# Routing of the first six token blocks moved from behind the first attention into it

## The chip, the cores and the metric

The kernel runs on one core of one Trainium2 chip. The metric is the time of one execution on the device in microseconds. The kernel before has a median of 1952.74 us over three runs (1950.49 to 1956.2).

## The reference

Four sequences of 1024 tokens of width 128 go through two layers, each with an attention and a feed-forward part, all added to the running x:

```
x = x + attn0(layernorm(x))   # causal, 16 heads of 8, softmax(q k / sqrt(128)), times Wo
x = x + moe(layernorm(x))     # router: softmax over 8 experts, top 2, weights renormalised
                              # expert: (silu(h @ gate) * (h @ up)) @ down, 128 -> 352 -> 128
x = x + attn1(layernorm(x))   # RMS norm, 16 query heads, 4 key heads, rope factor, not causal
x = x + ffn1(layernorm(x))    # 128 -> 512, a sine term, relu, 512 -> 128
```

The reference is float32. The change touches the place between attn0 and moe: for each token the two experts with the largest probability are found, and only those two are computed for it.

## The kernel before

The 4096 tokens are 32 tiles of 128, in eight blocks of four tiles (GT = 4, NG = 8). Two blocks are one sequence. Blocks 0 to 3 form routing group 0 and blocks 4 to 7 group 1.

**First attention.** It works through 16 head groups, g = 4 b + q: sequence b, heads 4q to 4q+3. While group g is finished, the row maxima of group g+1 and the first eight of g+2 are taken. Each group follows the string ORDERS[0], event by event, the same on TensorE, VectorE and ScalarE:
- "a", 32 per group: one unit of pass A. TensorE writes the scores of 128 queries against the keys up to them (pass_a, L766 and the mask L769). Unit i of eight has 128 (i+1) keys. VectorE takes their row maximum (row_max, L1441). The units use banks 0,1 and 2,3 of PSUM in turn, so pass_a of unit n waits until the row maximum of unit n-2 is taken. Units 0 to 3 of eight are at most 512 wide and so fill only bank 0 or bank 2.
- "b", 48 per group: pass B, the transposed scores with the maximum taken off (L799, L802), in one of three banks, and the exponential by ScalarE (L1179).
- "p", 12 per group: the product with V (pv, L815), four heads at once.
- "c" to "n": the output's copy (L1183), its turn (L831) and its division by the row sum (normalise_out, L1461 and L1466). That of a group's second half stands at the end of the string.

The last group, g = 15, has no pass A left, since there is no next one. Without it banks 0 to 3 are free there.

**Routing.** The dictionary ROUTE says at which step each engine does which part of a block. For group 0's table (key FIRST: blocks 0 to 5) a step below 12 stands at a PV event of the last head group; steps 12 to 25 run after attention(0), in a loop of each engine ("for step in range(LAYERS[0].G, LAST)"). Blocks 6 and 7 (LATE) are routed beside the first 39 expert tiles. The parts of one block are, on TensorE: T1 (turn of the attention output, L706), WO (product with Wo, L914), T2 (turn of the normed rows), LG (router logits, L919), PF (prefix counts, L924 and L926); on ScalarE: CP1, CP2 (copies out of the turn bank, L1210), EX (L1204); on VectorE: ADD (x plus the product, L1512, with the statistics L1356 and L1360), NORM (L1523), SH (L1531, L1534), RA (L1542 to L1550), RB (L1557 to L1566), RC (L1574, L1576), IDX (L1588 to L1594). TA and TB (L1605 to L1628) build the group's table of tiles: which expert each tile of 128 rows has and where its rows begin. Turns go to bank 1, all small results to bank 3.

**GpSimd** first fills the dispatch buffers (18 DMAs, L646, one after each of the first 18 half groups), then works through RS (inverse deviation, L567, L568) and the scatters: for each block 4 for the first choice (SA) and 4 for the second (SB), each an indirect DMA of 128 rows (L577). Blocks 4 and 5 are scattered beside the experts (steps 1, 3, 5, 7), and so are 6 and 7 (14, 16, 19, 21), four in a row each time.

**Experts.** 39 tiles of 128 rows per routing group, 78 in all. SyncE's queue loads a tile's rows and weights (L447, L448), eight tiles ahead at most, and only after the group's table and all its scatters. TensorE turns it (L940), multiplies by gate (L955) and up (L963), turns the product (L973) and multiplies by down (L983). ScalarE scales the result (L1235), and GpSimd scatters it back (L594) from one of four buffers (YS = 4); ScalarE waits for the landing of the scatter of four tiles before.

Most scratch tiles lie in the space of Q, which the attention uses until its end: slot q holds the queries of head group q.

Of the kernel before, what the change touches and what calls it, by code (L numbers as in the profile page):

```python
# [162 lines left out]
def steps(table, offsets, starts):  # L163

    for kind, offset in offsets:
        for u, start in starts.items():
# [4 lines left out]
FIRST = {0: 0, 1: 1, 2: 2, 3: 3, 4: 9, 5: 10}  # L171
LATE = {6: 0, 7: 4}
ROUTE = {
    "tensor": [steps({13: [("TOT", 0)]}, [("WO", 2), ("T2", 5), ("T1", 0), ("LG", 6), ("PF", 9)], FIRST),
               steps({20: [("TOT", 1)]}, [("T1", 1), ("WO", 2), ("T2", 6), ("LG", 7), ("PF", 12)], LATE)],
    "vector": [steps({13: [("TA", 0), ("TB", 0)]}, [("ADD", 2), ("NORM", 4), ("SH", 6), ("RA", 8), ("RB", 8), ("RC", 8), ("IDX", 9)], FIRST),
               steps({21: [("TA", 1)], 22: [("TB", 1)]},
                     [("ADD", 3), ("NORM", 5), ("SH", 8), ("RA", 9), ("RB", 10), ("RC", 11), ("IDX", 13)], LATE)],
    "scalar": [steps({}, [("CP2", 6), ("CP1", 1), ("EX", 7)], FIRST),
               steps({}, [("CP1", 1), ("CP2", 6), ("EX", 8)], LATE)],  # L180
    "gpsimd": [steps({}, [("RS", 2), ("SA", 10), ("SB", 10)], FIRST),
               steps({1: [("SA", 4)], 3: [("SB", 4)], 5: [("SA", 5)], 7: [("SB", 5)], 14: [("SA", 6)], 16: [("SB", 6)],
                      19: [("SA", 7)], 21: [("SB", 7)]}, [("RS", 3)], LATE)],
}
for step, found in ROUTE["gpsimd"][0].items():
    ROUTE["gpsimd"][0][step] = [(kind, u) for kind, u in found if kind == "RS" or u < GU]
LAST = 26
# [12 lines left out]
READS = numbers("vector", ("ADD", "SH", "IDX", "TA"))  # L200
COPIES = numbers("scalar", ("CP1", "CP2"))
assert [({"WO": "ADD", "LG": "SH", "PF": "IDX", "TOT": "TA"}[k], u) for k, u in SMALL] == list(READS)
assert [({"T1": "CP1", "T2": "CP2"}[k], u) for k, u in TURNS] == list(COPIES)
EARLY_TURNS = len(FIRST) * 2
EARLY_SMALL = len(FIRST) * 3 + 1
# [4 lines left out]
def build(nc, h_in, Wqvk, Wo0, router_w, gate_proj, up_proj, down_proj, w_q, w_k, w_v, w_o, g_rms,  # L210
# [9 lines left out]
    with ExitStack() as ctx:  # L220
# [24 lines left out]
        def part(at, *dims):  # L245
# [3 lines left out]
            if len(dims) == 3:  # L249
# [4 lines left out]
        rows = [part(0, GU, GT, ROW), probs[:, :, :].rearrange("p s n -> p (s n)")[:, 0:GU * GT * ROW]  # L254
                .rearrange("p (a b c) -> p a b c", a=GU, b=GT)]
        gated, acts, hT_tile = part(2304, 2, F0), part(3008, 2, F0P), part(3776, 2, P)
        actsT = part(5248, 2, len(FCH), P)
        x_tile, y_tile = part(6144, TS, P), part(4096, YS, P)
        done_e, pick_e = part(7168, TILES, E), part(7168 + TILES * E, TILES, E)
# [42 lines left out]
        tokens2 = sb("tokens2", [P, GT, D])  # L302
# [43 lines left out]
        cmp1 = sb("cmp1", [P, GT, E, E])  # L346
        cmp2 = sb("cmp2", [P, GT, E, E])
# [8 lines left out]
        y = sb("y", [P, GT, D])  # L356
# [68 lines left out]
        def _(sp):  # L425
# [7 lines left out]
            def load_tile(g, t):  # L433
# [97 lines left out]
        def _(pool):  # L531
# [38 lines left out]
            def scatter_rows(u, choice):  # L570

                v = u % GU
                pool.wait_ge(pre["indexed"], u + 1)
                apart(pool)
                for k in range(GT):
                    at = bass.IndirectOffsetOnAxis(ap=index[:, v, choice, k:k + 1], axis=0)
                    pool.indirect_dma_start(dispatch[u // GU][:, :], at, rows[u // GU][:, v, k, :], None)\  # L577
                        .then_inc(scattered[v], 16)

            def route(g, step):  # L580
                for kind, u in ROUTE["gpsimd"][g].get(step, ()):
                    if kind == "RS":
                        inverse(pre["stats"], pre["rstd"], u, rtmp_r[:, u, :], mv_r[:, u, :, 1], rstd_r[:, u, :])
                    else:
                        scatter_rows(u, 0 if kind == "SA" else 1)
# [56 lines left out]
            for n in range(NGRP * (E + 1) * CAP // (FILL * P)):  # L642
                g, c = n % NGRP, n // NGRP
                pool.wait_ge(s[0]["attn_done"], n + 1 + AT_ONE)
                place_of = dispatch[g][c * FILL * P:(c + 1) * FILL * P, :].rearrange("(p r) w -> p (r w)", p=P)
                pool.dma_start(place_of, some).then_inc(filled, 16)  # L646
            pool.wait_ge(filled, 16 * NGRP * (E + 1) * CAP // (FILL * P))
            for step in range(LAST):
                route(0, step)
            pool.wait_ge(s[0]["attn_done"], 2 * NQ + AT_ONE)  # L650
# [51 lines left out]
        def _(pe):  # L702
# [47 lines left out]
            def attention(l):  # L750
# [98 lines left out]
                def batch(b, final):  # L849
                    for q in range(4):  # L850
# [3 lines left out]
                        for ev in hd.events:  # L854
                            if ev[0] == "B":
                                pass_b(g, q, ev[1], ev[2])
                            elif ev[0] == "A":
# [6 lines left out]
                                if more_1:  # L864
                                    borrowed(k, g)
                                if k < 24 and more_1:
                                    pass_a(g + 1, (q + 1) % 4, 1 + k // 8, k % 8)
                                if k >= 24 and more_2:
                                    if k == 24:
                                        quad_loaded(b + (q >= 2), (q + 2) % 4)  # L870
                                    pass_a(g + 2, (q + 2) % 4, 0, k % 8)
                            elif ev[0] == "PV":
                                pv(g, q, ev[1])
                                if final and q == 3 and l == 0:
                                    pe.wait_ge(sl["max_done"], 32 * NQ)
                                    route(0, ev[1])
                                elif final and q == 3 and ev[1] in EARLY["tensor"][l]:
# [18 lines left out]

            def route(g, step):

                first, second = ((1, 3), (6, 7))[g]
                for kind, u in ROUTE["tensor"][g].get(step, ()):  # L900
                    if kind in ("T1", "T2"):
# [4 lines left out]
                        else:  # L906
                            pe.wait_ge(pre["normed"], u + 1)
                            turn(rows[u // GU][:, u % GU, :, 0:D], first, pre["turned"])
# [168 lines left out]

            for step in range(LAYERS[0].G, LAST):
                route(0, step)
# [13 lines left out]
        def _(act):  # L1093
# [61 lines left out]
            def attention(l):  # L1155
# [12 lines left out]
                def batch(b, final):  # L1168
                    for q in range(4):
                        g = 4 * b + q  # L1170
                        for ev in hd.events:
# [13 lines left out]
                            elif ev[0] == "PV" and final and q == 3 and l == 0:  # L1185
                                route(0, ev[1])
# [80 lines left out]
            for step in range(LAYERS[0].G, LAST):  # L1267
                route(0, step)
# [49 lines left out]
        def _(dve):  # L1318
# [116 lines left out]
            def attention(l):  # L1435
# [39 lines left out]
                def batch(b, final):  # L1475
                    for q in range(4):
                        g = 4 * b + q
                        more_1, more_2 = not (final and q == 3), not (final and q >= 2)
                        for ev in hd.events:
# [8 lines left out]
                            elif ev[0] == "PV" and final and q == 3 and l == 0:  # L1488
                                route(0, ev[1])
# [18 lines left out]
            def add_out(u, n, second):  # L1508
# [5 lines left out]
                statistics(u, pre["stats"], mv_r[:, u, :, :])  # L1514

            def norm_rows(u):

                v = u % GU
                dve.wait_ge(pre["rstd"], u + 1)
                if u >= GU:  # L1520
                    dve.wait_ge(s[0]["attn_done"], 2 * NQ + AT_ONE)
                for k in range(GT):
                    last = dve.tensor_scalar(rows[u // GU][:, v, k, 0:D], x[:, u * GT + k, :], mv_r[:, u, k, 0:1],  # L1523
                                             rstd_r[:, u, k:k + 1], ALU.subtract, ALU.mult)
                last.then_inc(pre["normed"], 1)
# [11 lines left out]
            def compare_experts(u):  # L1537

                par = u % 2
                dve.wait_ge(pre["exped"], u + 1)  # L1540
                probs_e = exped[:, par, :, :]
                own.done(dve.tensor_reduce(r1[:, :], probs_e, AX, ALU.add))  # L1542
                own.done(dve.reciprocal(r2[:, :], r1[:, :]))
                own.done(dve.tensor_tensor(rc[:, :, :], probs_e, over_e(r2[:, :]), ALU.mult))
# [36 lines left out]
            def place_rows(u, n, second):  # L1581
# [3 lines left out]
                if u >= GU:  # L1585
                    dve.wait_ge(scattered[v], 16 * 2 * GT)
# [239 lines left out]
```

## Time and profile before

| what | us |
|---|---|
| median of three runs | 1952.74 |
| the profiled execution, device time | 1953.41 |
| its span, first to last instruction | 1951.6 |
| PE busy | 1739.1 (89%) |
| DVE busy | 1380.9 (71%) |
| ACT busy | 1131.4 (58%) |
| POOL busy | 303.0 (16%) |
| mean granted TensorE clock | 0.930 |

PE is TensorE, DVE VectorE, ACT ScalarE, POOL GpSimd, SP SyncE; PEld is the load of weights on TensorE. Busy time leaves out waits. In rows of the timeline the first number is the start, the second the time that the merged instructions took, and the bracket the idle time before them and who ended it. In rows of a stretch the busy time of each engine stands with its count of instructions, then the granted clock (1.00 is 2.4 GHz, 0.50 is 1.2 GHz), the DMA share and GB/s.

### The profile page before, as it was taken

To read this page: it belongs to the slowest core of one execution; us is meant where nothing else is said; L and a number is where in the kernel's file an instruction comes from. 1 tells how busy PE (TensorE), PEld (TensorE's weight loads), DVE (VectorE), ACT (ScalarE), POOL (GpSimd) and SP (SyncE) were. 2 spreads that over 40 slices of the span, in tenths; PEclk is the share of its full clock that TensorE was granted. 3 is DMA by queue.
4 is the path that set the end of the run, shared out by engine and by line. 5 is a ranking of instruction groups with operands and counts; after the bars stand their busy time and mean duration, and the time that the engine had idled before them with its cause. 6 is when DMAs were issued, how large, how long until landed. Compare 5 with 4: busy or idle time off the path is not lost.

```text
span 1951.6 us, 30989 instructions
## 1 busy us (share of the span) xinstructions
PE 1739.1 (89%) x10550; PEld 726.1 (37%) x10550; DVE 1380.9 (71%) x2363; ACT 1131.4 (58%) x2396; POOL 303.0 (16%) x387
## 2 busy tenths in 40 slices
PE   4599999999998456898878999999999999999886
PEld 2234444444443244565521222222222222222365
DVE  6577777777774645446489788888888888884386
ACT  3246666666666123333341677777777777777776
POOL 4100000000001454435350000000000000000265
PEclk9679999999999578899965999999999999999998
DMA  7635443424200011122142011111111111000000
GB/s 212 152 64 120 112 120 111 129 78 50 35 2 2 29 58 50 50 65 66 55 124 32 2 20 19 19 20 18 19 19 20 17 17 17 2 2 1 1 17 27
DMA packets 109098, 96.27 MB, mean 49 GB/s; under 512 B 58478, under 2 KB 86771, under 8 KB 106640
## 3 DMA queue, kind: packets, MB, share of 16 engines
q1 hardware_dynamic: 91104, 48.02, 15.0%
q0 software_dynamic: 10208, 40.39, 5.6%
q10 hardware_dynamic: 7632, 5.88, 1.1%
q8 instruction: 88, 1.44, 0.3%
q14 instruction: 66, 0.54, 0.1%
HBM read 48.03 MB, written 43.38 MB: 47 GB/s over the span
## 4 chain that ended last, share of the span: by engine, by line
PE 73%; issue 8%; DVE 7%; ACT 4%; POOL 2%; DMA 2%; ACTq 1%; another core or an unknown queue 1%; SPq 0%; POOLq 0%; DVEq 0%
PE ps L815 21%; PE ps L799 18%; PE ps L766 18%; DVE rowmax L1441 3%; PE ps L983 2%; PE ps L963 2%; PE ps L955 2%; DMA k_parts<-Q 2%; PE ps L831 2%; ACT probs L1179 2%; PE ps L973 2%; PE ps L769 1%; PE ps L802 1%; ACTq L1096 1%
## 5 line engine op out<-in xcount | busy, mean ns | idle before, releaser
L1441 DVE TENSOR_REDUCE rowmax<-ps 128x1 f32<-128x1024 f32 (+7 forms) x1024 | 970.0, 987 | 245.5 <-PE ps L766 125.1
L1179 ACT ACTIVATE probs<-ps 128x512 f32<-128x512 f32 (+3 forms) x1792 | 857.8, 556 | 345.6 <-PE ps L799 216.5
L766 PE MATMUL ps<-K,Q 72*128 72x512 bf16 (+3 forms) x1792 | 539.6, 376 | 25.3 <-DVE rowmax L1441 21.7
L799 PE MATMUL ps<-Q,K 75*128 75x512 bf16 (+3 forms) x1792 | 537.6, 362 | 12.3 <-ACT probs L1179 8.4
L815 PE MATMUL ps<-probs,V 128*9 128x512 f32 (+3 forms) x3584 | 446.1, 555 | 0.0
L799 PEld LDWEIGHTS ps<-Q,K 75*128 75x128 bf16 x1792 | 166.0, 98 | 361.5 <-ACT probs L1179 263.4
L766 PEld LDWEIGHTS ps<-K,Q 72*128 72x128 bf16 x1792 | 152.7, 99 | 312.8 <-DVE rowmax L1441 164.0
L1661 DVE TENSOR_TENSOR Q<-ps,Q 128x352 f32<-128x352 f32 x78 | 40.9, 524 | 122.5 <-ACT Q L1226 90.5
L567 POOL TENSOR_SCALAR rtmp<-mv 128x4 f32<-128x4 f32 x8 | 1.9, 233 | 808.3 <-DVE mv L1360 808.3
L815 PEld LDWEIGHTS ps<-probs,V 128*9 128x9 f32 x3584 | 61.2, 89 | 146.8 <-ACT probs L1179 84.8
L769 PE MATMUL ps<-causal,identb 128*128 128x128 bf16 x512 | 115.1, 228 | 0.0
L802 PE MATMUL ps<-identb,causal 128*128 128x128 bf16 x512 | 105.3, 223 | 0.0
L1235 ACT ACTIVATE Q<-ps,meta 128x128 f32<-128x128 f32 x78 | 28.6, 367 | 127.0 <-PE ps L983 95.1
L594 POOL DMA_INDIRECT returned<-Q,target x78 | 77.9, 999 | 116.9 <-ACT Q L1235 97.2
L983 PE MATMUL ps<-wd,Q 128*128 (+1 forms) x468 | 68.0, 283 | 4.5 <-issue 3.9
L963 PE MATMUL ps<-wu,Q 128*128 x156 | 66.3, 508 | 0.0
L769 PEld LDWEIGHTS ps<-causal,identb 128*128 128x128 bf16 x512 | 51.6, 101 | 39.3 <-issue 5.5
L1183 ACT ACTIVATE oT<-ps 128x512 f32<-128x512 f32 x64 | 38.4, 600 | 45.7 <-PE ps L815 45.7
L706 PE MATMUL ps<-ident,tokens 128*128 128x128 f32 x128 | 23.1, 310 | 44.9 <-DVE tokens L1393 32.7
L955 PE MATMUL ps<-wg,Q 128*128 x156 | 62.5, 483 | 0.5 <-ACT Q L1218 0.5
L983 PEld LDWEIGHTS ps<-wd,Q 128*128 128x128 f32 (+1 forms) x468 | 60.5, 197 | 6.0 <-issue 5.7
L646 POOL DMA_DIRECT2D dispatch<-wg x18 | 9.7, 536 | 316.8 <-DVE attn L1466 316.8
(226 smaller groups left out, 1484.8 us busy)
## 6 DMA issues: line engine op xcount, KB each, us to landing
dispatch<-wg POOLq DMA_DIRECT2D x18, 1152.0 KB, 8.7
Q<-q_parts SPq DMA_DIRECT2D x288, 64.0 KB
K<-k_parts SPq DMA_DIRECT2D x144, 64.0 KB
q_parts<-Q POOLq DMA_DIRECT2D x16, 384.0 KB, 3.7
Q<-dispatch SPq DMA_DIRECT2D x78, 64.0 KB
probs<-returned SPq DMA_DIRECT2D x8, 512.0 KB
k_parts<-Q POOLq DMA_DIRECT2D x8, 384.0 KB, 7.4
V<-v SPq DMA_DIRECT2D x16, 144.0 KB
```

The source lines that it names most:

```text
L594: pool.indirect_dma_start(returned[:, :], at, y_tile[:, k, :], None, bounds_check=2 * B * S - 1, oob_is_err=False).then_inc(tile_out[k], 16)
L766: last = pe.matmul(buf[:, c:e], Q[0:CROSS, slot, j, i * P:(i + 1) * P], K[0:CROSS, slot, kj, c:e], start=True, stop=not diag)
L769: last = pe.matmul(buf[:, w - P:w], identb[:, :], causal[:, :], start=False, stop=True)
L799: last = pe.matmul(ps[:, bank, c:HALF], K[0:KROWS, q, kj, t * P:(t + 1) * P], Q[0:KROWS, q, j, h * HALF + c:(h + 1) * HALF], start=True, s ...
L802: last = pe.matmul(ps[:, bank, c:c + P], causal[:, :], identb[:, :], start=False, stop=True)
L815: last = pe.matmul(ps[32 * j:32 * j + rows, PV_BANK, c:HALF], V[:, q, t, kj * rows:(kj + 1) * rows], probs[:, (4 * m + j) % PR, c:HALF], s ...
L955: pe.matmul(ps[:, par, 0:F0], hT_tile[:, par, :], wg[:, bass.ds(expert, 1), :].rearrange("p a f -> p (a f)"), start=True, stop=True).then_ ...
L963: pe.matmul(ps[:, 2 + par, 0:F0], hT_tile[:, par, :], wu[:, bass.ds(expert, 1), :].rearrange("p a f -> p (a f)"), start=True, stop=True).t ...
L983: last = pe.matmul(ps[:, 5, P:2 * P], actsT[0:w, n % 2, c, :], wd[0:w, c, bass.ds(expert, 1), :].rearrange("p a d -> p (a d)"), start=(c = ...
L1179: act.activation(probs[:, (4 * m + j) % PR, c:HALF], ps[:, B_BANKS[(4 * m + j) % 3], c:HALF], ACT.Exp, scale=SCALE).then_inc(sl["exp_done" ...
L1441: dve.tensor_reduce(rowmax[:, par, 8 * j + i:8 * j + i + 1], score_a(i % 2)[:, 0:hd.keys(i)], AX, ALU.max).then_inc(sl["max_done"], 1)
L1661: dve.tensor_tensor(acts[:, par, 0:F0], ps[:, 2 + par, 0:F0], gated[:, par, :], ALU.mult)\
```

## The change

"at(window, event)" is a place in pass A of the first attention: event k of 32 of head group g is place 32 g + k, and a window is eight places. EARLY_BLOCKS starts block u at window 32 + 4u, so one block per head group, and a block takes eight windows: the second half of one runs beside the first half of the next. The parts are the same instructions as before, cut finer: ADD loses its statistics to ST and AG, NORM becomes N1 and N2, RA/RB/RC become RA to RF and CA, CB, IDX loses its end to INT, and the table's TA and TB become TA to TG.

```diff
-FIRST = {0: 0, 1: 1, 2: 2, 3: 3, 4: 9, 5: 10}
-LATE = {6: 0, 7: 4}
+def at(window, event):
+    return 8 * window + event
+EARLY_BLOCKS = {0: at(32, 0), 1: at(36, 0), 2: at(40, 0), 3: at(44, 0), 4: at(48, 0), 5: at(52, 0)}
+LATE_BLOCKS = {6: 0, 7: 4}
...
+    "tensor": [steps({at(54, 1): [("TOT", 0)]},
+                     [("T1", at(0, 1)), ("WO", at(1, 1)), ("T2", at(3, 1)), ("LG", at(4, 1)), ("PF", at(7, 1))], EARLY_BLOCKS),
+               steps({21: [("TOT", 1)]}, [("T1", 1), ("WO", 2), ("T2", 6), ("LG", 7), ("PF", 13)], LATE_BLOCKS)],
+    "vector": [steps({at(54, 3): [("TA", 0)], at(54, 5): [("TB", 0)], at(54, 7): [("TC", 0)], at(55, 2): [("TD", 0)],
+                      at(55, 4): [("TE", 0)], at(55, 6): [("TF", 0)], at(56, 2): [("TG", 0)]},
+                     [("ADD", at(1, 3)), ("ST", at(1, 5)), ("AG", at(1, 7)), ("N1", at(2, 4)), ("N2", at(2, 6)),
+                      ("SH", at(4, 3)), ("RA", at(5, 0)), ("RB", at(5, 2)), ("RC", at(5, 4)), ("RD", at(5, 6)),
+                      ("RE", at(6, 0)), ("RF", at(6, 2)), ("CA", at(6, 4)), ("CB", at(6, 6)),
+                      ("IDX", at(7, 3)), ("INT", at(7, 5))], EARLY_BLOCKS),
...
+    "scalar": [steps({}, [("CP1", at(0, 2)), ("CP2", at(3, 2)), ("EX", at(4, 5))], EARLY_BLOCKS),
...
+    "gpsimd": [{}, steps({}, [("RS", 3)] + [(n, 15 + n) for n in range(2 * GT)], LATE_BLOCKS)],
...
+EARLY_ROWS = [("RS", 0), ("RS", 1), ("SC", 0), ("RS", 2), ("SC", 1), ("RS", 3), ("SC", 2), ("RS", 4), ("SC", 3),
+              ("RS", 5), ("SC", 4), ("SC", 5)]
```

On TensorE a routing part follows pass A of its place, and two waits give the banks back before the next wide unit:

```diff
+            def banks_back(step):
+                if step - 3 in TURN_AT:
+                    pe.wait_ge(pre["copied"], TURNS[TURN_AT[step - 3]] + 1)
+                if step - 4 in SMALL_AT:
+                    pe.wait_ge(pre["small_read"], SMALL[SMALL_AT[step - 4]] + 1)
```

VectorE does a part right after the row maximum of its place; ScalarE does one at the place of the "a" in its own order, between exponentials. The loops of steps behind attention(0) go, on all engines. The rows to be scattered get a tensor of their own for two blocks at a time, so a new wait stands before a block is normed:

```diff
+        rows = sb("rows", [P, 2, GT, ROW])
...
+                    if u >= 2:
+                        dve.wait_ge(scattered[(u - 2) % GU], 16 * 2 * GT * ((u - 2) // GU + 1))
```

GpSimd issues its 18 fills in the first 14 half groups ("(g * fills + c) * 7 // 9 + 1"), those of one dispatch buffer before those of the other, then EARLY_ROWS in order with eight scatters for each "SC". Blocks 6 and 7 are scattered one indirect DMA per tile and block, at steps 15 to 22 and 19 to 26. The experts' scratch tiles move into slots 0 and 1 of Q, and SyncE may load the first expert tiles once head group 12 is out of its slot:

```diff
                 if t == 0:
                     sp.wait_ge(pre["tables"], g + 1)
+                    sp.wait_ge(s[0]["o_turned"], 2 * (NQ - 3) + AT_ONE)
```

The comparison tiles cmp1, cmp2 and the table's done_e, pick_e share one tensor; tokens2 and y share the space of rows.

## Rows read from the trace of the kernel before

**Rows 1.** The page: busy tenths of PE and its granted clock in 40 slices.
```profile
PE   4599999999998456898878999999999999999886
...
PEclk9679999999999578899965999999999999999998
```
**Rows 2.** Stretches: one head group; after the last group's middle; layer 1's last group.
```profile
441.20:473.40 32.20, 31.85 (x266) 14.40 (x265) 24.36 (x40) 21.07 (x52) 0.00 (x0) 1.00 0.36 43
...
640.00:704.00 64.00, 21.19 (x129) 15.20 (x125) 44.68 (x199) 6.41 (x18) 35.24 (x38) 0.55 0.11 38
...
1787.10:1834.20 47.10, 41.70 (x243) 13.34 (x241) 7.90 (x33) 35.38 (x69) 2.43 (x4) 1.00 0.00 1
```
**Rows 3.** Timeline: thirtieth half group's division (VectorE), the first expert tile (TensorE).
```profile
601.20 0.29 DVE L1466 TENSOR_TENSOR attn<-ps,rden 128x128 f32<-128x128 f32 x1
...
704.10 0.45 PE L940 MATMUL ps<-ident,Q 128*128 128x128 f32 x1 [2.38 <-DMA meta<-dispatch]
```
**Rows 4.** GpSimd's scatters of rows: duration min/median/max in ns, first and last start.
```profile
L577 POOL DMA_INDIRECT dispatch<-Q,index x32: 957/962/1151, 654.3 to 697.2; - x32
```
**Rows 5.** VectorE's row maxima in 441.2 to 473.4, by width: busy, mean ns, idle before.
```profile
L1441 DVE TENSOR_REDUCE rowmax<-ps 128x1 f32<-128x1024 f32 x4 | 4.9, 1218 | 0.2 <-PE ps L769 0.2
...
L1441 DVE TENSOR_REDUCE rowmax<-ps 128x1 f32<-128x896 f32 x4 | 4.3, 1084 | 0.2 <-PE ps L769 0.2
...
L1441 DVE TENSOR_REDUCE rowmax<-ps 128x1 f32<-128x768 f32 x4 | 3.8, 950 | 0.1
...
L1441 DVE TENSOR_REDUCE rowmax<-ps 128x1 f32<-128x640 f32 x4 | 3.3, 822 | 1.2 <-PE ps L769 1.1
...
L1441 DVE TENSOR_REDUCE rowmax<-ps 128x1 f32<-128x512 f32 x4 | 2.8, 688 | 1.1 <-PE ps L769 1.0
...
L1441 DVE TENSOR_REDUCE rowmax<-ps 128x1 f32<-128x384 f32 x4 | 2.2, 555 | 2.9 <-PE ps L769 2.9
...
L1441 DVE TENSOR_REDUCE rowmax<-ps 128x1 f32<-128x256 f32 x4 | 1.7, 419 | 1.1 <-PE ps L769 1.1
...
L1441 DVE TENSOR_REDUCE rowmax<-ps 128x1 f32<-128x128 f32 x4 | 1.1, 287 | 0.9 <-PE ps L769 0.9
```
**Rows 6.** Waits in 441.2 to 473.4: us in total, times, longest.
```profile
PEld ps L766 <- DVE rowmax L1441: 3.3, 6, 0.9
```
**Rows 7.** Timeline of VectorE: first and last instructions of routing parts.
```profile
610.84 0.69 DVE L1512 TENSOR_TENSOR x<-x,ps 128x512 f32<-128x512 f32 x1 [9.35 <-PE ps L914]
...
612.61 0.38 DVE L1360 BATCH_NORM_AGGREGATE mv_r<-stats 128x2 f32<-128x6 f32 x4
...
621.71 1.08 DVE L1523 TENSOR_SCALAR Q<-x,mv_r,rstd_r 128x128 f32<-128x128 f32 x4
...
647.12 0.19 DVE L1531 TENSOR_REDUCE r<-ps 128x4 f32<-128x32 f32 x1
...
653.26 0.17 DVE L1594 CAST index<-index_f 128x8 int32<-128x8 f32 x1
...
674.63 0.16 DVE L1605 COPY total<-ps 128x8 f32<-128x8 f32 x1
...
680.96 0.18 DVE L1628 TENSOR_SCALAR skip<-t_row 128x39 int32<-128x39 f32 x1
```
**Rows 8.** Timeline of TensorE: a turn, the product with Wo, the logits.
```profile
607.29 0.63 PE L706 MATMUL ps<-ident,attn 128*128 128x128 f32 x4
...
609.64 1.16 PE L914 MATMUL ps<-wo,aT 128*128 128x128 f32 x8
...
627.89 0.96 PE L919 MATMUL ps<-wr,hT 128*128 128x8 f32 x8
```
**Rows 9.** Stretches with the expert turns (L940) alone: PE and PEld with counts, clock.
```profile
719.50:743.60 24.10, 1.19 (x4) 0.56 (x4) 0.91 0.23 63
...
766.50:805.00 38.50, 2.34 (x7) 1.05 (x7) 0.78 0.18 53
805.00:892.00 87.00, 9.88 (x33) 4.52 (x33) 1.00 0.23 61
```

More of the change, by code:

```diff
@@ L185 @@
-for step, found in ROUTE["gpsimd"][0].items():
-    ROUTE["gpsimd"][0][step] = [(kind, u) for kind, u in found if kind == "RS" or u < GU]
-LAST = 26
+    "tensor": [steps({at(54, 1): [("TOT", 0)]},
[7 more added lines that the diff above has]
+                      ("IDX", at(7, 3)), ("INT", at(7, 5))], EARLY_BLOCKS),
+               steps({22: [("TA", 1), ("TB", 1)], 23: [("TC", 1), ("TD", 1)], 24: [("TE", 1), ("TF", 1)], 25: [("TG", 1)]},
+                     [("ADD", 3), ("ST", 3), ("AG", 3), ("N1", 5), ("N2", 5), ("SH", 8), ("RA", 9), ("RB", 9), ("RC", 10),
+                      ("RD", 10), ("RE", 11), ("RF", 11), ("CA", 12), ("CB", 12), ("IDX", 14), ("INT", 14)], LATE_BLOCKS)],
@@ L200 @@
 READS = numbers("vector", ("ADD", "SH", "IDX", "TA"))
+TURN_AT = {step: ev for step, found in ROUTE["tensor"][0].items() for ev in found if ev in TURNS}
+SMALL_AT = {step: ev for step, found in ROUTE["tensor"][0].items() for ev in found if ev in SMALL}
 COPIES = numbers("scalar", ("CP1", "CP2"))
@@ L574, in scatter_rows, with inverse_rows @@
                 apart(pool)
[L575 to L578, printed above, removed]
+                to = bass.IndirectOffsetOnAxis(ap=index[:, v, n // GT, n % GT:n % GT + 1], axis=0)
+                pool.indirect_dma_start(dispatch[u // GU][:, :], to, rows[:, u % 2, n % GT, :], None)\
+                    .then_inc(scattered[v], 16)
+            def inverse_rows(u):
+                inverse(pre["stats"], pre["rstd"], u, rtmp_r[:, u, :], mv_r[:, u, :, 1], rstd_r[:, u, :])
             def route(g, step):
@@ L907, in route @@
                             pe.wait_ge(pre["normed"], u + 1)
-                            turn(rows[u // GU][:, u % GU, :, 0:D], first, pre["turned"])
+                            turn(rows[:, u % 2, :, 0:D], first, pre["turned"])
                         continue
@@ L1076, in _ @@
             attention(0)
-            for step in range(LAYERS[0].G, LAST):
-                route(0, step)
             experts()
@@ L1576, in count_picks @@
+            def count_picks(kind, u):
+                v = u % GU
+                if kind == "CA":
+                    if v == 0:
+                        own.done(dve.memset(count[:, v, 0, :], 0.0))
+                    else:
+                        own.done(dve.tensor_copy(count[:, v, 0, :], count[:, v - 1, GT, :]))
+                for k in ((0, 1) if kind == "CA" else (2, 3)):
                     last = dve.tensor_tensor(count[:, v, k + 1, :], count[:, v, k, :], picked[:, v, k, :], ALU.add)
@@ L1578, in count_picks @@
                         own.done(last)
-                tell(last, pre["picked"], u + 1)
+                    else:
+                        tell(last, pre["picked"], u + 1)
             def place_rows(u, n, second):
```

252 lines of the change are left out of this document (131 added, 121 removed).

## The prediction

> **What bounds the kernel now.** I read first the 40 slices: PE is at 9 tenths in both attentions, and between them stands a hole at the slices from 12 to 16, where PE falls to 4 to 8 tenths and its granted clock with it [rows 1]. Then the stretches. A head group of the first attention takes 32.2 us with PE busy 31.85, VectorE 24.36, ScalarE 21.07 [rows 2]: PE sets the pace there. From 640 to 704 PE is busy 21.2 of 64 us at a mean clock of 0.55 while VectorE works 44.7 and GpSimd 35.2 [rows 2]: that is the routing, alone. Then two single events: group 14 is divided at 601.20, and the first expert tile turns at 704.10 [rows 3], 102.9 us for what is only one more head group and the routing. GpSimd's 32 scatters of blocks 0 to 3 run from 654.3 to 697.2, about 1.3 us each with the gap [rows 4], and the tile loads wait for the last of them, so at the end it is this queue that releases the experts. Last the experts: from 805 on, 33 tiles in 87.0 us, 2.64 each, at clock 1.00; but 4 tiles in 24.1 us and 7 in 38.5 us in two stretches before [rows 9].
>
> **What goes.** The time from 601.20 to 704.10 becomes one bare last group. PE no longer has pass A there, so ScalarE sets it: 48 exponentials and two copies, 21.07 us in a full group [rows 2]. Layer 1's last group, without pass A too, took 47.1 us for 35.4 of ScalarE's work, 1.33 times [rows 2]; the same ratio gives 28, ScalarE alone 21. I take 26.5, and 0.5 for the handover; the tile loads are then long under way, since SyncE's queue has nothing else in the last group, and GpSimd's eight scatters of block 5 end inside it. So the experts start at 628.2 + X, where X is what the moved work adds to groups 8 to 14. Gain here: 704.1 - 628.2 - X = 75.9 - X.
>
> **What it adds to the attention, X.** Per block, on VectorE: ADD, ST and AG from 610.84 to 612.99, 2.15; N1 and N2 1.08; SH, RA to CB, IDX and INT from 647.12 to 653.43, 6.3 with their gaps [rows 7]. Together 9.55 us. VectorE's idle time in a group is 32.2 - 24.36 = 7.8, so that 1.7 cannot fit even if all were used; and it is not all usable. The idle before a row maximum depends on its width: 0.9, 1.1, 2.9, 1.1 and 1.2 us per group (four windows) before units 0 to 4, but 0.1, 0.2 and 0.2 before units 5 to 7 [rows 5]. PE has no spare either: pass A already waits 3.3 us per group for a row maximum [rows 6], and with two buffers each late row maximum is a late pass A, behind which all of pass B and pv stand in PE's fixed order. So I match each piece with the idle behind its place, a fourth of the group's:
> - behind units 4, 5 and 6 stand N1 with CA (1.1), RC (0.9), ST (0.9), INT (0.4), N2 with CB (0.9) and RD (0.65), 4.85 in all, with 0.03 to 0.05 of idle each: 4.6 stays;
> - behind units 0, 2 and 3 stand RA, RE, RB, RF, ADD, SH, IDX, 4.25 in all, with 0.3 each: 2.2 stays;
> - AG behind unit 7, 0.4 against 0.2: 0.2 stays. The widest hole, 0.7 before unit 2, gets no piece.
>
> That is 7.0. On PE a block adds two turns of 0.63, 1.16 for Wo, 0.96 for the logits [rows 8] and, as an estimate, 0.4 for the prefix counts: 3.8. Most of it (the turns, Wo) falls in windows in which VectorE is then the later engine; I let 1.1 of it through. ScalarE's two bank copies and small exponential come between exponentials; with 11 us idle per group it pays them itself. So 8 us per block, 48 for six.
> The table's VectorE work runs from 674.63 to 681.14, 6.5 us [rows 7]; in seven pieces, against the same idle, 5 stays. X = 53. Bounds: below, PE's own work with VectorE's all hidden, 6 x 3.8 = 23; above, nothing hidden and each bank copy as long as a turn waited for: 6 x (9.55 + 3.8 + 1.3) + 6.5 = 94. I stand nearer the middle because of the idle before narrow units [rows 5].
>
> **The new waits.** VectorE's N1 of block u waits for the scatters of block u-2; the row maxima are queued behind it and PE behind them. Block u-2's index is ready at its window 7.6, and N1 comes at 10.5 of the same count: 2.9 windows of some 10 us, 29 us, for eight scatters of 1.3 [rows 4] and an inverse, 12 us. It costs nothing; were that cover gone, each us late would be a us of PE. PE's waits for the banks stand before units 4 and 5, whose pass A waits for the row maximum of unit 2 or 3 anyway; ADD (0.7) may make the one later, and that is in the 7.0. The 18 fills go faster by two ninths, on queues that share the attention's loads; hidden, since PE is at 9 tenths where they run already [rows 1]. GpSimd has 48 scatters in the attention, 62 us, in a queue that was idle there.
> Against hiding GpSimd's work speaks a rule. The slowest of the 32 scatters took 1151 ns, the median 962, though VectorE was busy 44.7 of 64 us at that time [rows 2, 4]. The Trainium skill, page "SBUF — State Buffer", section "SBUF: two separate sides", says that a DMA issued by GpSimd starves while VectorE holds their shared port in a two-port mode, and that 620 ns became about 3100. This case's trace does not show it to that extent. If it held, an estimate by the page's figure puts a block's scatters at some 27 us, just within those 29; the sum would be later by at most a few us per block.
>
> **The experts' first half.** In the stretch from 719.5 to 743.6, four tiles took 24.1 where 2.64 each make 10.6: 13.5 over; from 766.5 to 805 seven took 38.5 instead of 18.5: 20 over [rows 9]. In both GpSimd scatters four rows of a block at a time, 5.1 us, in front of the tiles' own scatters, whose landing frees ScalarE's buffers. The first burst goes (blocks 4 and 5 are done); I leave 3 us for the routing of blocks 6 and 7 there. The second is spread: one extra scatter per tile makes 1.3 + 1.3 = 2.6, the pace of PE, and only in steps 19 to 22, with two, GpSimd is late by 1.3 each, 5 us; with the table 6.5. Gain 33.5 - 9.5 = 24; bounds 15 (bursts cheaper than their stretches look) and 31. Part of it is the clock, which should stay at 1.00.
>
> **Sum.** Span 1951.6 - (75.9 - 53) - 24 = 1904.7. Around the span lie 1953.41 - 1951.6 = 1.8, giving 1906.5 against that execution; the median of the runs was 0.7 less than it, so 1906.
>
> **Rivals.**
> - *The pieces hide.* Routing rides in VectorE's idle and PE's slack, X = 30: 1883. For it: 7.8 us idle per group. Against: the idle is before narrow units, pieces also stand behind wide ones.
> - *Lock-step.* VectorE, PE and ScalarE wait in turn, each part a round trip, X = 80: 1933. For it: two buffers and three banks leave hardly any slack [rows 6]; the old stretch from 640 to 704 shows how such a chain runs. Against: inside the attention other work stands between the parts.
> - *The experts are held up by something else*, for example by GpSimd being late with its chain or by the landing of the scatters: the start gains 20 us less and the spreading only 15 in place of 24: 1935.
> - *The other side: the clock.* The holes that VectorE makes in PE's work let the granted clock fall to 0.50 in the routed groups, as it did behind the attention (0.55 in the mean) [rows 2]. A group's 31.85 + 3.8 of PE work would become up to 71 us in place of about 40, 31 more; 1.5 such groups (46.7 us) eat the gain, beyond 1.7 it is slower than can be told from noise, and two give 1968. For it: PE would be idle about a tenth of the time. Against: 41.70 busy of 47.10 kept a clock of 1.00 [rows 2], and routed groups should have 35.6 of 40.
>
> **How the numbers follow.** My forecast 0.60, hidden 0.13, lock-step 0.16, held up 0.05, clock 0.06. The forecast's own range is 1893 to 1921. The range for 8 in 10 takes in the hidden case and the lock-step: 1881 to 1940. What a measurement of this kernel can tell from no change is about 0.3%, 5.9 us. Faster than 1946.9: all of the first two, nearly all of the third and fourth, 0.91; slower, 0.05 from the clock; 0.04 between, from the tail of lock-step (X above 93).
>
> **What would show it.** Groups 8 to 13 at about 40 us in place of 32.2, group 14 at about 36, groups 0 to 7 as before; in the routed groups pass A's wait for the row maximum well above 3.3 us and VectorE busy about 33 us; PE busy near 36 at clock 1.00. The group 14 division at about 654, the first expert turn 27 us behind it. GpSimd's scatters of blocks 0 to 5 about 1.3 us each, ended before the experts; first 25 expert tiles in about 77 us instead of 101. Wrong would be: routed groups near 36 or above 45, a stretch at 0.50 inside the attention, tile loads later than the last group, a last group other than 24 to 29 us, VectorE found idle before N1 for GpSimd, or waits of 5 us and more for the landing of the experts' scatters, as before.

## The result and the profile after

The change was 1.1% slower: 1973.99 us in the median of four runs (1971.44 to 1982.24) against 1953.18 us (1950.49 to 1956.2) for the kernel before beside it, ratio 1.0113, 95% interval 1.0078 to 1.0149. Forecast was 1906. The profiled execution has a span of 1969.9 us at a mean granted clock of 0.933.

The kernels of one comparison ran on one chip, and the kernel before was run again beside them. That turned out to matter, and the answer stands here in one table; "held" says whether the profiles of that comparison show the stall that the sections below are about.

| comparison | kernel before, us | held | kernels and their ratio to the kernel before (95% interval) |
|---|---|---|---|
| 1 | 1953.18 | yes | the change 1.0113 (1.0078 to 1.0149) |
| 2 | 1952.37 | yes | no_scatter 0.982 (0.9794 to 0.9846); burst_indirect 1.0233 (1.0204 to 1.0261); burst_direct 1.0009 (0.9993 to 1.0026); spread2 0.9861 (0.9837 to 0.9885) |
| 3 | 1954.67 | yes | spread_all 0.9811 (0.9789 to 0.9833); spread_late 0.9815 (0.9767 to 0.9862); burst4 1.0006 (0.9988 to 1.0023); burst_landed 1.0008 (0.9987 to 1.0029) |
| 4 | 1921.23 | no | burst6 1.002 (1.0002 to 1.0038); burst8_half 1.002 (1.0002 to 1.0038); change_landed 1.0027 (1.0014 to 1.004) |
| 5 | 1923.05 | no | the change again, change_b, 0.9874 (0.9843 to 0.9905); burst_indirect_b 0.9987 (0.9963 to 1.0011); burst6_b 1.0022 (1.0005 to 1.004); spread_all_b 0.9845 (0.9819 to 0.9871) |
| 6 | 1923.2 | no | burst6_c 1.0008 (0.9985 to 1.0032); burst8_half_c 0.9994 (0.9973 to 1.0015) |

The page after, which answers to [rows 1]: the hole behind the attention is gone, but PE is now at 7 to 8 tenths in slices 9 to 14 (counted from 0), and PE's clock dips in most of them.
```profile
PE   4599999998878879799977999999999999999887
...
POOL 4100000001111113535360000000000000000265
PEclk9679999998898889899965899999999999999998
```

The stretches, in the columns of [rows 2]. The first is head group 9, the first with a full load of routing; the second is group 10; the third group 14. Each begins some 1.4 us behind the division that ends the group before:
```profile
411.80:451.80 40.00, 35.68 (x292) 16.76 (x292) 32.09 (x80) 22.71 (x55) 3.47 (x5) 1.00 0.29 36
451.80:503.50 51.70, 41.81 (x294) 19.32 (x293) 32.44 (x80) 23.48 (x55) 9.29 (x11) 0.83 0.26 39
...
658.70:706.80 48.10, 36.22 (x245) 14.29 (x245) 24.08 (x59) 20.78 (x51) 12.55 (x14) 0.78 0.09 28
```
Group 9 is as forecast (about 40 us, PE near 36, VectorE about 33, clock 1.00): 40.0 us, PE 35.7, VectorE 32.1, clock 1.00. From group 10 on, with the same work for PE, VectorE and ScalarE, a group takes 51.7, 51.6, 48.6, 55.1 and 48.1 us, at half clock for part of each. What group 10 has and group 9 lacks is POOL's work: 9.29 us against 3.47. GpSimd's first eight scatters start at 449.0, the next eight at 500.6, then 552.2, 600.7, 654.7 and 691.6. Answering to [rows 3], the thirtieth division comes at 705.41 (601.20 before) and the first expert tile at 735.28 (704.10 before):
```profile
705.41 0.29 DVE L1489 TENSOR_TENSOR attn<-ps,rden 128x128 f32<-128x128 f32 x1
...
735.28 0.33 PE L968 MATMUL ps<-ident,Q 128*128 128x128 f32 x1 [0.68 <-DVE attn L1489]
```

The timeline of the second burst shows what happens (start, duration, instruction, and in the bracket the idle time with who ended it):
```profile
505.74 0.22 PE L788 MATMUL ps<-causal,identb 128*128 128x128 bf16 x1
...
507.00 0.95 POOL L588 DMA_INDIRECT dispatch<-rows,index  x1 [0.30 <-issue]
...
508.25 0.96 POOL L588 DMA_INDIRECT dispatch<-rows,index  x1 [0.30 <-issue]
508.64 0.49 ACT L1204 ACTIVATE probs<-ps 128x384 f32<-128x384 f32 x1 [4.78 <-remote]
...
509.19 0.50 PE L818 MATMUL ps<-Q,K 75*128 75x384 bf16 x1 [2.50 <-issue]
...
509.52 0.95 POOL L588 DMA_INDIRECT dispatch<-rows,index  x1 [0.30 <-issue]
512.34 1.16 DVE L1464 TENSOR_REDUCE rowmax<-ps 128x1 f32<-128x384 f32 x2 [8.66 <-remote]
512.42 0.87 ACT L1204 ACTIVATE probs<-ps 128x384 f32<-128x384 f32 x2 [2.80 <-remote]
```
PE's mask product of the 384-wide unit, the last instruction of its pass A, ended at 505.96. VectorE's row maximum of that unit, which waits for it, started at 512.34, 6.4 us later, after 8.66 of idleness that the view can put down to no engine ("remote"). ScalarE has such waits of 4.78 and 2.80 in the same microseconds. The trace also keeps the time of every semaphore update, and there the lateness stands directly. From 440 to 735 PE's updates come 0.01 us behind the end of their instruction in the median, but 33 of 562 come more than 1 us behind it, up to 7.9; of ScalarE's and VectorE's none is 0.1 us late. The rows show it too: ScalarE's exponential ended at 509.13 and PE's next product, which waits for it, began at 509.19, in the middle of VectorE's wait. So what is late is PE's word to the others, and they stand still; I call it the hold. (The ends of matmuls are modelled, so whether the results or only the updates come late is not told apart.) The waits of the whole attention from 440 to 735 (us in total, times, longest), "remote" alone:
```profile
DVE rowmax L1464 <- remote: 33.5, 6, 8.7
...
ACT probs L1204 <- remote: 20.4, 6, 4.8
...
ACT oT L1208 <- remote: 8.4, 1, 8.4
```
In the trace before, no row maximum and no exponential of the attention has such a wait. The granted clock falls to 0.50 (1.2 GHz) 4 to 11 us after the first scatter of each burst: for 17.1, 17.1, 6.8, 13.7, 10.2 and 13.7 us from 457.3, 508.5, 563.1, 610.9, 658.7 and 696.2. One more fall, of 3.4 us at 645.0, stands near no burst. The scatters themselves are as short as in [rows 4]:
```profile
L588 POOL DMA_INDIRECT dispatch<-rows,index x64: 954/958/1122, 449.0 to 832.5; - x64
```

The experts, from the first turn to the start of the 26th: 88.1 us, where the trace before has 103.5 (704.1 to 807.6):
```profile
735.30:823.40 88.10, 7.78 (x25) 3.60 (x26) 0.94 0.16 43
```

### The profile page after: what moved, and what is told of

Its sections match the earlier page's. It is cut to its first block, busy times and chain, and to the rows that moved or that the text cites. A ratio compares the mean times of both kernels' runs of the same rounds, so it can differ in the third digit from the quotient of the medians.

```text
span 1969.9 us, 31128 instructions
## 1 busy us (share of the span) xinstructions
PE 1755.3 (89%) x10550; PEld 723.3 (37%) x10550; DVE 1376.7 (70%) x2363; ACT 1135.5 (58%) x2396; POOL 302.7 (15%) x387
## 4 chain that ended last, share of the span: by engine, by line
PE 69%; DVE 13%; ACT 5%; issue 3%; another core or an unknown queue 3%; POOL 2%; DMA 2%; ACTq 1%; SPq 0%; POOLq 0%; DVEq 0%
PE ps L834 19%; PE ps L818 17%; PE ps L785 17%; DVE rowmax L1464 8%; PE ps L1011 2%; PE ps L991 2%; PE ps L983 2%; ACT probs L1204 2%; DMA k_parts<-Q 2%; PE ps L1001 2%; PE ps L850 2%; PE ps L821 1%; ACTq L1121 1%; PE ps L788 1%
## 5 line engine op out<-in xcount | busy, mean ns | idle before, releaser
L785 PE MATMUL ps<-K,Q 72*128 72x512 bf16 (+3 forms) x1792 | 547.6, 380 | 64.4 <-DVE rowmax L1464 53.8
L818 PE MATMUL ps<-Q,K 75*128 75x512 bf16 (+3 forms) x1792 | 543.8, 365 | 19.7 <-ACT probs L1204 8.6
L1260 ACT ACTIVATE Q<-ps,meta 128x128 f32<-128x128 f32 x78 | 28.6, 367 | 123.5 <-PE ps L1011 87.2
L588 POOL DMA_INDIRECT dispatch<-rows,index x64 | 62.0, 968 | 123.2 <-DVE index L1634 104.5
L1208 ACT ACTIVATE oT<-ps 128x512 f32<-128x512 f32 x64 | 38.4, 600 | 65.3 <-PE ps L834 56.9
L1484 DVE RECIPROCAL rden<-ps 128x16 f32<-128x16 f32 x64 | 16.0, 250 | 68.5 <-PE ps L850 68.3
```

Of the source, the lines that this page charges most:

```text
L588: pool.indirect_dma_start(dispatch[u // GU][:, :], to, rows[:, u % 2, n % GT, :], None)\
L785: last = pe.matmul(buf[:, c:e], Q[0:CROSS, slot, j, i * P:(i + 1) * P], K[0:CROSS, slot, kj, c:e], start=True, stop=not diag)
L818: last = pe.matmul(ps[:, bank, c:HALF], K[0:KROWS, q, kj, t * P:(t + 1) * P], Q[0:KROWS, q, j, h * HALF + c:(h + 1) * HALF], start=True, s ...
```

## Experiments

Theory A: eight indirect DMAs queued by GpSimd hold back the semaphore updates that the other engines wait for, and the clock falls with the hold. Rivals: B, VectorE's routing parts and the waits in lock-step cost it themselves; C, the scatters collide with SyncE's loads; D, any burst of DMAs on GpSimd's queue does it. The expectations use the same letters.

**Take the scatters out.** Blocks 0 to 5 are not dispatched, so the experts work on zero rows; four more fills, to another tensor, make up for the DMAs taken out.
```diff
-                    for n in range(2 * GT):
-                        scatter_rows(u, n)
+                    pool.wait_ge(pre["indexed"], u + 1)
...
-                    if u >= 2:
-                        dve.wait_ge(scattered[(u - 2) % GU], 16 * 2 * GT * ((u - 2) // GU + 1))
```


> The changed kernel without the 48 early scatters of blocks 0 to 5 (the rows of those blocks are not dispatched; four more fills write the return buffer instead, so that it is defined). Theory A, the scatters themselves stop the other engines: groups 10 to 13 come down from 51.6, 51.5, 48.7 and 55 us to about 40, 40, 40 and 46, group 14 to about 39, no wait of 4 us and more on anything in the attention, clock 1.00 there; about 1925 us. Theory B, the parts on VectorE and their round trips cost more than the 8 us per block as soon as two blocks overlap: groups 10 to 13 stay near 50, above 1960 us. Theory C, the scatters collide with SyncE's loads of the next group: as A.

1913.75 us, 0.982. Groups 8 to 14: 35.1, 40.1, 40.1, 41.3, 40.1, 43.7, 35.0 us; no "remote" wait from 440 to 660; first expert tile at 675.9. Two stretches of 40 us, most of groups 9 and 10:
```profile
401.00:441.00 40.00, 36.09 (x299) 16.81 (x291) 31.85 (x75) 23.35 (x57) 1.28 (x2) 1.00 0.30 35
441.00:481.00 40.00, 35.62 (x295) 16.81 (x291) 32.21 (x79) 22.66 (x55) 1.29 (x2) 1.00 0.30 35
```
All routing on VectorE and PE is still there. B falls: with the scatters the first expert tile comes 59 us later (735.3 against 675.9); 3 of these lie before the first division, so 56 are the scatters'.

**Put scatters into the kernel before.** Five bursts of eight, to a scratch tensor, at the starts of groups 10 to 14; the second kernel has the same bytes as direct DMAs.
```diff
+            for b in range(5):
+                pool.wait_ge(s[0]["attn_done"], 2 * (10 + b) + AT_ONE)
+                apart(pool)
+                for k in range(8):
+                    at = bass.IndirectOffsetOnAxis(ap=idx_c[:, k:k + 1], axis=0)
+                    pool.indirect_dma_start(scratch[:, :], at, rows_c, None).then_inc(burst_sem, 16)
+                pool.wait_ge(burst_sem, 16 * 8 * (b + 1))
```
In the second kernel this stands in place of the two lines with "at":
```diff
+                    pool.dma_start(scratch[k * P:(k + 1) * P, :], rows_c).then_inc(burst_sem, 16)
```


> The kernel before, plus five bursts of eight indirect DMAs of 128 rows to a scratch buffer, issued by GpSimd at the start of groups 10 to 14. Nothing waits for them. A: each of these groups goes from 32.3 (30.9 for group 14) to 40 to 44 us, with the same waits of 4 to 9 us on nothing that the profile names; 1995 to 2010 us. B: no change, 1953 us. C: as A in groups 10 to 12, where SyncE loads, and nothing in groups 13 and 14.

> The same five bursts with direct DMAs of the same 128 rows of 576 bytes, also by GpSimd. If what hurts is the indirect kind (A in its narrow form): groups stay at 32.3, 1953 us. If it is any burst on GpSimd's queue, or the collision of its packets with SyncE's loads (C): like the indirect bursts, 1980 us and more. B: 1953 us.

Indirect: 1996.13 us, 1.0233; the five groups took 38.4, 41.7, 43.1, 41.0 and 39.7 us instead of 32.3 and 30.9. Direct: 1954.74 us, 1.0009, groups 32.3 and 30.9 as without. Group 10 with its burst, first indirect (with its "remote" waits), then direct:
```profile
438.70:477.10 38.40, 34.12 (x267) 14.88 (x265) 24.60 (x41) 21.76 (x52) 7.83 (x8) 0.96 0.34 51
...
DVE rowmax L1452 <- remote: 5.1, 2, 3.3
ACT probs L1190 <- remote: 4.5, 1, 4.5
```
```profile
441.90:474.20 32.30, 31.95 (x267) 14.40 (x265) 24.44 (x41) 21.17 (x52) 4.26 (x8) 1.00 0.38 61
```
So the hold needs nothing of the change, and it is not bytes (D falls). C falls too: in groups 13 and 14 SyncE starts one transfer each, at 597 and 638, 34 us behind the first scatter of the burst, and they lost 8.8 and 8.7 us, as much as the others.

**Never eight back to back.** First two units of pass A between scatters, with block 5 left as a burst; then block 5 paced too, by ScalarE's exponentials in the last group (the edit shown); then blocks 6 and 7 at one scatter per tile.
```diff
                     for n in range(2 * GT):
+                        if u < 5:
+                            pool.wait_ge(s[0]["max_done"], 40 + EARLY_BLOCKS[u] + at(7, 6) + 2 * n)
+                        else:
+                            pool.wait_ge(s[0]["exp_done"], 3 + 4 * LAYERS[0].G * (NQ - 1) + 4 + 5 * n)
                         scatter_rows(u, n)
```


> The changed kernel, but GpSimd lets two units of pass A pass between the scatters of a block (eight scatters over 16 units, some 20 us in place of 10). A, if the harm comes from scatters queued back to back: the standstills of 8.7 us per block vanish or shrink to about 1 us, groups 10 to 13 near 42, about 1930 us. A, if each scatter stops the others for its own time: the sum of the stops is the same, about 1970 us. B: no change, 1974 us.

> The changed kernel with two units of pass A between scatters for blocks 0 to 4, as in spread2, and five exponentials of the last group between those of block 5, which in spread2 still went in one burst. If queued scatters are the harm: no wait of 9 us in group 14 or the last group; groups 10 to 13 at 40.1 and 43.7 as in spread2; group 14 35 to 45 (its half clock of 23.9 us in spread2 followed a wait of 4.0 us that may come again), last group 28; 1908 to 1918 us. If the parts on VectorE were at fault in group 14: 1925 us as spread2.

> spread_all, and in the experts' first half blocks 6 and 7 are scattered one after the other, one indirect DMA per tile at steps 15 to 30, never two. If queued scatters cost there too (intervals of 5.2, 5.8, 4.1 and 6.8 us against 2.64 in spread2), the first 39 tiles take 4 to 8 us less than in spread_all; if the two per tile only delay the tiles' own scatters, about 3 us less.

spread2: 1925.03 us, 0.9861; groups 10 to 13 at 40.1 to 43.7, and block 5's burst in group 14 still made one wait of 9.1 us of ScalarE on "remote", group 14 being 52.9. spread_all: 1914.93 us (1910.69 to 1915.09), 0.9811, faster than both kernels; groups 9 to 12 at 40.1, group 13, which has the table too, at 44.9, group 14 at 36.2, no "remote" wait from 440 to 735, first expert tile at 676.5. The same 48 scatters run in it. Groups 10 and 11:
```profile
445.00:485.10 40.10, 35.75 (x291) 16.81 (x291) 32.19 (x81) 22.76 (x54) 9.21 (x11) 1.00 0.34 49
485.10:525.20 40.10, 35.75 (x291) 16.83 (x291) 32.19 (x81) 22.76 (x54) 9.04 (x11) 1.00 0.34 50
```
POOL's 9.2 us are as in the change's group 10, and the 51.7 us are 40.1. spread_late: 1914.21 us, no gain over spread_all (39 expert tiles in 127.0 us against 127.1): its experts still had seven "remote" waits of ScalarE, 22.6 us, the longest 3.5. There a block's scatter stands behind the tiles' own, one by one, and some hold remains; so eight in a row are not the only thing that brings it, and what does in the experts is open.

**How many, and queued or landed.** Bursts of four in the kernel before; eight, each issued when the one before has landed.


> The kernel before plus five bursts at the start of groups 10 to 14, as in burst_indirect, but of four indirect DMAs each. If each indirect DMA costs the other engines its share, the five bursts cost half of burst_indirect's 43.8 us: 1974 us. If the harm comes only once several are queued (the first waits in burst_indirect begin some 4 us after its first DMA), four cost little: groups 32.3 to 34 us, 1953 to 1960 us.

> The five bursts of eight indirect DMAs, but each one is issued only when the one before has landed. If it is their standing in the queue behind each other that stops the others: groups stay at 32.3 us (30.9 for group 14), 1953 us. If it is the number of them in a short time, whatever the order: near 1996 us, or in between as the pace is slower.

burst4: groups 33.0, 33.5, 33.5, 32.6, 31.3 us, 3.9 us in all, 1.0006. burst_landed: groups 32.3, the last two 32.5 and 30.7, 1.0008. Here eight scatters that wait for each other's landing cost nothing, and four queued ones little. But waiting for the landing also halves their pace (2.5 us from one to the next in place of 1.3), so whether the queue or the pace matters is not told apart. And a landing can be late:
```profile
452.46 0.98 POOL L658 DMA_INDIRECT scratch<-wg,idx_c  x1 [8.40 <-DMA scratch<-wg,idx_c]
462.44 0.96 POOL L658 DMA_INDIRECT scratch<-wg,idx_c  x1 [9.00 <-DMA scratch<-wg,idx_c]
464.99 0.96 POOL L658 DMA_INDIRECT scratch<-wg,idx_c  x1 [1.58 <-DMA scratch<-wg,idx_c]
```

**Six, eight of 64 rows, and the change with each scatter after the landing of the one before.**


> As burst_indirect, with six indirect DMAs per burst. Four cost 3.3 us over five groups, eight cost 43.8. If the cost sets in with the fifth in the queue and grows with each one: about 20 us, 1973 us. If it is a step at eight: below 5 us, 1957 us.

> As burst_indirect, eight indirect DMAs per burst, but of 64 rows each, so half of the rows. If what fills up is counted in rows or their descriptors: like four whole ones, 1953 to 1958 us. If it is counted in instructions: like eight, 1996 us.

> The changed kernel, where each early scatter of a block waits until the one before it has landed, and nothing else. From burst_landed: no standstill, groups 10 to 12 at 40.1 where every scatter lands within about 3 us. But there two of eight took 9 us to land behind SyncE's loads, so a block's eight may need 30 us, and VectorE's norm of the block after next waits for them: groups 10 to 12 at 40 to 44. 1908 to 1925 us. If the standstills came from anything but queued scatters: 1974 us.

Here the kernel before took 1921.23 us, and neither of the first two profiles has a "remote" wait anywhere from 440 to 865, the experts included, where every profile of comparisons 2 and 3 has at least 15 us of them on ScalarE alone. So they tell nothing of the threshold: groups 32.3 in both. Why both are 0.2% slower than the kernel before was not followed up. (The 3.3 us that the expectation gives for bursts of four are 3.9 by the groups above.) change_landed took 1928.75 us, 1.0027, with groups 10 to 12 at 53.7, 52.0 and 51.5 us (40 to 44 expected) although nothing was held. Its group 10 and its waits:
```profile
446.10:499.80 53.70, 38.41 (x293) 17.80 (x293) 32.49 (x80) 22.86 (x54) 9.17 (x11) 0.84 0.25 37
```
```profile
POOL dispatch L588 <- DMA dispatch<-rows,index: 29.0, 7, 13.0
...
DVE rows L1557 <- POOL rstd_r L580: 11.3, 1, 11.3
```
That is another route to the same loss: GpSimd waits 29.0 us for the landings of one block's scatters, it is late with the next block's chain, VectorE's N1 waits 11.3 us for it, and the row maxima stand behind N1. Pacing by landing loses here what the spreading gains; with the hold it was not run.

**Is the hold there on every chip?** The change unaltered, bursts of eight and of six, and the spread version in one comparison. In these expectations N says that the hold is on every chip, H that it depends on the chip.


> The change as it is, in one call with the three kernels below, so that all four share a chip. Theory N (a queue of eight scatters holds the other engines' semaphore updates on every chip): 1.0% slower than the kernel before, groups 10 to 14 at 48 to 55 us. Theory H (the hold depends on the chip; where the kernel before takes about 1921 us instead of 1953 it is absent): if the kernel before takes about 1953 here, as N; if it takes about 1921 here, every routed group at 40.1 us and about 1888, ratio 0.983.

> The kernel before with five bursts of eight queued indirect DMAs at the start of groups 10 to 14. It was 2.3% slower where the kernel before took 1953 us. N: 2.3% slower again, the five groups at 38 to 43 us. H: 2.3% slower if the kernel before takes about 1953 us here, within 0.3% and groups at 32.3 us if it takes about 1921.

> The same with bursts of six. Where the kernel before takes about 1953: if the hold grows with the number in the queue, between bursts of four (+0.06%, groups +0.7 each) and of eight (+2.3%, groups +8.8 each), so +0.8 to +1.5%; if six still fit, within 0.3%. Where it takes about 1921: within 0.3%, as it was there, and then only theory H or N is told apart, by the run of eight beside it.

> The change with its early scatters spread over each group, never eight in the queue. N: 2.0% faster than before and 3% faster than the change beside it. H, chip with before at 1953: the same; chip with before at 1921: within 0.3% of the change beside it, since there is no hold for the spreading to take away, and both about 1.7% faster than before.

The kernel before took 1923.05 us, and the change was 1.3% faster (1901.73 us, 0.9874; H had expected 1888). Not one "remote" wait stands in its profile from 440 to 735, no update of PE comes 0.1 us late, and its groups 9 to 12 took 40.0 to 40.1, though the bursts are the same (from 449.1, 489.2, 529.3, ...). Groups 11 to 14, nearly:
```profile
489.00:529.10 40.10, 35.74 (x292) 16.82 (x291) 32.19 (x80) 22.77 (x55) 9.10 (x10) 1.00 0.33 50
529.10:569.20 40.10, 35.73 (x292) 16.81 (x291) 32.19 (x80) 22.77 (x55) 9.11 (x10) 1.00 0.29 50
569.20:614.60 45.40, 38.15 (x306) 17.93 (x304) 38.45 (x99) 24.46 (x58) 11.04 (x12) 1.00 0.05 17
614.60:658.00 43.40, 41.15 (x252) 17.31 (x253) 25.20 (x62) 21.16 (x51) 9.12 (x10) 0.72 0.06 20
```
burst_indirect_b, 2.3% slower in comparison 2, was 0.9987 here; its group 10 (38.4 us above):
```profile
441.70:474.00 32.30, 31.95 (x267) 14.41 (x265) 24.40 (x41) 21.16 (x52) 7.81 (x8) 1.00 0.40 61
```
spread_all_b took 1895.54 us, 0.9845: its interval (0.9819 to 0.9871) overlaps the change's, so the spreading costs nothing and gains nothing sure where there is no hold. Two kernels ran once more, for the threshold:

> The kernel before with bursts of six queued indirect DMAs of 128 rows at the start of groups 10 to 14. Where the kernel before takes about 1953 us beside it (a chip with the hold): if the hold begins with the count of queued instructions or of queued rows, groups between bursts of four (+0.7 us each) and of eight (+8.8 each): +2 to +6 each, 0.5 to 1.5% slower; if six still fit, within 0.3%. Where the kernel before takes about 1921: within 0.3%, and nothing is told apart.

> The same with bursts of eight of 64 rows each, so as many rows as in a burst of four whole ones. Where the kernel before takes about 1953: if the queued rows decide, as bursts of four: within 0.3%; if the number of queued instructions decides, as bursts of eight: 2.3% slower, groups at 38 to 43 us. Where it takes about 1921: within 0.3%, nothing told apart.

Again a kernel before of 1923.2 us, and groups 32.3 (30.9 for group 14). The threshold between four and eight, and whether queued instructions or queued rows count, stay open.

## Why the prediction was wrong

- **X, what the routing adds to groups 8 to 14: right for the routing itself.** Forecast 53; in the change it was 105.5, by the divisions at 375.3 and 705.41. In no_scatter it is 50.6 (2.8 + 7.8 + 7.8 + 9.0 + 7.8 + 11.4 + 4.0 over 32.28 and 30.94), in spread_all 52.1, in change_b 57.9. The eight per block were 7.8, VectorE's 33 were 32.1, PE's 36 were 35.7. In change_b group 14 took 43.3 instead of 36, 23.9 us of it at half clock, from a fall at its start, right behind group 13, in which VectorE had 38.5 of 45.4 us of work. spread2 (23.9 us) and spread_all_b (30.7) have it in the same place, no_scatter and spread_all only 3.4 and 6.8 us of it. So the clock rival was real for one group in some runs; what decides it was not found.
- **"In a queue that was idle there", hidden: the step that failed.** GpSimd's 48 scatters were costed by their own 62 us and by who waits for their landing, and so put at nothing. I had asked what they delay downstream, not what they do to engines that need nothing of them. The bursts stood VectorE still for up to 8.7 us at a time, the clock fell for up to 17.1 us with them, and the first expert tile came 56 us later than with none. The rival with the half clock was near in size (1968 against 1974), and that is luck: it puts the fall down to the holes that VectorE's parts make, and these leave the clock at 1.00 in group 9; with the hold it is 0.83 in group 10. A long wait of another kind does the same: 0.84 in change_landed's group 10.
- **The rule weighed there, against the runs.** The scatters kept their 958 ns in the median beside a busy VectorE, so the starving of GpSimd's DMAs that the Trainium skill (page "SBUF — State Buffer", section "SBUF: two separate sides") describes does not appear. Whether VectorE was in such a mode here the trace does not say; in spread_all, where it is busy for 32.2 of 40.1 us, the median is 958 ns too. The harm went the other way, from the queued DMAs to the engines.
- **The last group: 26.5 + 0.5 forecast, 28.2 to 29.5 measured** for the group and 28.6 to 29.9 from the division to the first tile, over all runs of the changed kernel and its variants. The start of the tile loads was hidden, as forecast: the first expert tile waits for VectorE's last division (0.68), no longer for a DMA.
- **The experts' first half: 24 forecast, 13 measured.** 39 tiles took 140.4 us before, 127.4 after. The sign and the cause by "bursts" were right, the size was not: where nothing is held, a kernel with the experts of the kernel before (burst6_b) takes 115.4 for the same tiles and change_b 110.3, a gain of 5. (From the first to the 25th turn 77 us were forecast in place of 101; it was 84.3, and 70.5 in change_b.) Most of the excess in [rows 9] was the hold under the kernel's own scatters, and after the change blocks 6 and 7 still have theirs. In the trace before it could be seen (ScalarE, 704 to 805), and I took it for landings:
```profile
ACT Q L1235 <- remote: 23.0, 4, 9.8
```
- **The sum.** In the change the first tile came 31.2 us later where 22.9 earlier were forecast, and the experts' first half gave 13.0 of 24: the span grew by 18.3 (1951.6 to 1969.9) where 46.9 less were forecast. Without the hold in the attention the steps give most of what they promised: spread_all's 1914.93 beside a kernel before of 1954.67 is a gain of 39.7 where 46.7 were forecast. By the spans (1951.6 and 1908.9) it is 42.7: 27.6 at the start (22.9 forecast; 5.4 of the 27.6 lie before the first division and are not the change's), 13.3 in the experts, 1.8 behind them. Where nothing is held at all the change gains 21.3, since the kernel before is itself 30 us faster there, 25 of them in these 39 tiles (140.4 against 115.4).

That the hold makes the loss is shown (scatters out, in, spread, landed, and the same kernels with and without it). That PE's updates are what is late is read from their times in the traces; why queued indirect DMAs should do it, and why on some chips, was not found. Whether it is the chip or something else that stays constant over a comparison is not told apart either: three comparisons have it and three do not, and no chip was used twice in 2 to 6.

## What to carry to other kernels

An instruction in an idle queue can still cost the busy engines: before moving a row of indirect DMAs beside tuned work, look in the old trace at what the engines did while such DMAs ran, "remote" waits above all, and space them by other work (here two units) instead of issuing eight back to back. Where a kernel's time differs by 1.6% from one comparison to another, a single comparison on one chip gives no verdict on a change: the same edit was 1.1% slower and 1.3% faster.

## What the hardware showed that was not expected

- Where there is a hold, eight indirect DMAs of 128 rows, 1.3 us apart, cost a tuned attention group 6 to 11 us (comparison 2); four cost 0.3 to 1.2 (comparison 3); eight direct ones of the same bytes nothing; eight that each wait for the landing of the last nothing.
- The hold is in TensorE's semaphore updates: up to 7.9 us late in the change's attention. From 440 to 865 no update of ScalarE is 0.1 us late in any profile, and at most one of VectorE's is more than 1 us late. In the profiles without the hold no update of TensorE is 0.1 us late there either.
- The kernel before runs in 1952 to 1955 us beside kernels that show the hold and in 1921 to 1923 beside those that do not.
- A scatter that follows the landing of the last waited 1.6 us mostly and 8.4 to 12.7 for four of burst_landed's 40.
- VectorE with 32.1 of 40.0 us busy, and PE with 35.7, kept the granted clock at 1.00.
